# Two-layer mixed network on eight cores: the q/k normalisation and rotation of the last block issued one chunk later

## The reference

```python
h = shift_token(x)            # second half of the features delayed by one token
qkv = h @ wqkv
q, k, v = jnp.split(qkv, 3, axis=-1)
# to 8 heads of 64
q = l2norm(q) * qs            # l2norm(t) = t / clip(norm(t), 1e-12)
k = l2norm(k) * ksc
q, k = rotary_xpos(q, k)      # q * cos * scale + rotate_half(q) * sin * scale; k likewise with 1/scale
o = local_attention(q, k, v)  # window 512
```

## Time and profile before

| what | us |
|---|---|
| median of 2 runs | 26131.15 (26050.67 and 26211.63) |
| the profiled execution | 26278.76 |
| its span, slowest core (core 3) | 26277.2 |
| shortest core span of the same execution | 26008.6 |
| mean granted TensorE clock, slowest core | 0.615 of full |

### The profile page before, as it was taken

How to read it: one execution, slowest core, us unless ns; L and a number is a source line. 1 busy time by engine, 2 the same in 40 slices (tenths; PEclk the granted TensorE clock), 3 DMA queues, 4 the chain that set the end, 5 groups by cost and what they waited for, 6 DMA issues and landing times.

```text
span 26277.2 us, 172792 instructions; the slowest of 8 cores (26008.6 to 26277.2 us)
## 1 busy us (share of the span) xinstructions
PE 12685.6 (48%) x43266; PEld 5477.6 (21%) x43266; DVE 8884.8 (34%) x21875; ACT 4131.0 (16%) x6863; POOL 2171.6 (8%) x2737
## 2 busy tenths in 40 slices
PE   1212215771443344434443443444568777778773
PEld 0111112220111122222222222222211133211231
DVE  4444443334333333333333333332232222322222
ACT  0111111111212211111111111110123211233110
POOL 0010010000000000000000000000014300034000
PEclk7555557885666665555555555555775688755786
DMA  2111113333000010010001001001211101111103
GB/s 70 34 22 36 36 21 63 65 64 101 20 16 15 19 37 2 2 25 2 2 3 25 2 3 25 2 3 37 57 36 37 56 31 44 34 39 43 48 19 96
DMA packets 1067639, 849.03 MB, mean 32 GB/s; under 512 B 770196, under 2 KB 888756, under 8 KB 1064372
## 3 DMA queue, kind: packets, MB, share of 16 engines
q1 hardware_dynamic: 923572, 492.83, 7.8%
q0 software_dynamic: 143104, 345.14, 4.7%
HBM read 445.31 MB, written 302.25 MB: 28 GB/s over the span
## 4 chain that ended last, share of the span: by engine, by line
PE 45%; DVE 24%; issue 10%; ACT 8%; SPq 5%; DMA 5%; POOL 1%; DVEq 1%; another core or an unknown queue 0%; ACTq 0%; POOLq 0%; PEldq 0%
PE a_pU L1395 4%; PE ffc_pA L2175 3%; PE ffc_pG L2183 2%; PE ffc_pY L2203 2%; PE a_pZ L1388 2%; PE a_psQ L1162 2%; PE a_pJ L1390 2%; PE ffa_pP L1764 2%; DVE a_rrow L945 2%; PE a_psW L1167 2%; PE ffb_pO L1946 1%; DVE a_Gp L1392 1%; DVE a_phs L844 1%; PE ffb_pD L1948 1%; PE ffb_pS L1960 1%
## 5 line engine op out<-in xcount | busy, mean ns | idle before, releaser
L1395 PE MATMUL a_pU<-a_Zs,a_Hp 128*128 128x128 f32 x2560 | 980.5, 487 | 971.8 <-DVE a_Hp L1394 971.8
L1972 POOL TENSOR_TENSOR ffb_p<-ffb_e,ffb_mask 128x512 bf16<-128x512 bf16 x960 | 1093.1, 1150 | 965.2 <-ACT ffb_e L1966 523.2
L1449 ACT ACTIVATE a_sqO<-a_Osb 128x256 f32<-128x256 f32 x256 | 106.9, 418 | 6165.0 <-DVE a_Osb L1434 6070.2
L1395 PEld LDWEIGHTS a_pU<-a_Zs,a_Hp 128*128 128x128 f32 x2560 | 640.7, 311 | 1311.6 <-issue 1311.6
L1388 PE MATMUL a_pZ<-a_Gp,a_Hp 128*128 128x128 f32 x2560 | 845.7, 434 | 139.5 <-DVE a_Hp L1383 139.5
L2175 PE MATMUL ffc_pA<-ffc_hn,ffc_w 128*128 128x512 bf16 x2816 | 730.6, 407 | 295.6 <-DVE ffc_hn L2162 295.6
L1475 POOL DMA_DIRECT2D a_og<-a_OgB x256 | 137.9, 539 | 8393.1 <-DVE a_tE L1357 7180.0
L1390 PE MATMUL a_pJ<-a_Hp,a_Gp 128*128 128x128 f32 x2560 | 812.0, 421 | 0.0
L1397 DVE TENSOR_TENSOR a_Zs<-a_Zs,a_pU 128x128 f32<-128x128 f32 x1280 | 368.5, 288 | 1307.6 <-PE a_pU L1395 1299.4
L1964 DVE TENSOR_SCALAR ffb_cl<-ffb_pS 128x512 f32<-128x512 f32 x624 | 429.8, 691 | 957.1 <-PE ffb_pS L1960 565.2
L1946 PE MATMUL ffb_pO<-ffb_p,ffb_v 128*64 128x512 bf16 x960 | 597.0, 622 | 294.9 <-POOL ffb_p L1972 270.5
(11 more groups left out here) (395 smaller groups left out, 24637.6 us busy)
## 6 DMA issues: line engine op xcount, KB each, us to landing
moe_w<-l_w POOLq DMA_DIRECT2D x64, 1024.0 KB, 14.2
ln_x<-x SPq DMA_DIRECT2D x64, 512.0 KB, 3.8
a_phq<-a_phs SPq DMA_DIRECT2D x64, 512.0 KB, 3.8
f_xatt<-ffb_xo POOLq DMA_DIRECT2D x128, 256.0 KB, 2.3
ffc_w<-f_w SPq DMA_DIRECT2D x2, 11264.0 KB
ffc_x<-f_xatt SPq DMA_DIRECT2D x72, 256.0 KB, 4.5
xn_bf<-ln_o POOLq DMA_DIRECT2D x64, 256.0 KB, 2.3
s<-a_s POOLq DMA_DIRECT2D x32, 512.0 KB, 2.9
```

What stands on the lines that cost most here:

```text
L1395: zm = seq.step("tensor", lambda eng: nc.tensor.matmul(pU[:, 0:128], Hp[:], Zs[:], start=True, stop=True), deps=[he, zj, prev.get(("pU", 0))])
L1972: msk = seq.step("gpsimd", lambda eng, am=am, ma=ma: eng.tensor_tensor(psb[am][:], ebf[am][:], maskb[:, 512 * ma:512 * (ma + 1)], ALU.mult ...
```

## The change

The steps of a q/k chunk from the square to the store move into a function `emit_qk_tail`, and the loop calls it one chunk later: `mmR` and `mmS` of a chunk are called, then the tail of the chunk before, and the chunk's own arguments are kept in `pend_qk`. The tail of the tile's last k chunk is called after `mmR`, the copy and the store of the first v chunk. No instruction's operands, shape or number changes, and no buffer is added; what the tail's steps wait for stays as it was, with the counters `sb2` and `ao` advanced when the tail is called.

```diff
+        pend_qk = None
+        last_rot = None
...
             last_mm = None
             last_rot = None
+            def emit_qk_tail(pp, pp2, tb, scol, toff, oc, dst, t0, tld, mm_r, mm_s):
+                nonlocal pr_rw, pr_rv, pr_bc, pr_rotbb, pr_bbread, gsq, gao, last_rot
+                sb2 = gsq % 2; gsq += 1
+                sqs = seq.step("scalar", lambda eng, sb2=sb2, pp=pp: eng.activation(
+                    sqsb[sb2][:], psP[pp][:], AF.Square), deps=[mm_r] + list(pr_sqc[sb2]))
...
+                bc = seq.step("tensor", lambda eng: (
+                    nc.tensor.matmul(psBB[0:64, :], onesr[0:1, 0:64], rsA2[:], start=True, stop=True),
+                    nc.tensor.matmul(psBB[64:128, :], onesr[0:1, 0:64], rsB2[:], start=True, stop=True))[-1],
+                    deps=[rv, pr_rotbb])
...
+                rot = seq.step("vector", rotk, deps=[bbe, mm_r, mm_s, tld, qsld, ini, pr_aost[ao]])
+                last_rot = rot
...
+                pr_ppc[pp] = (sqs, rot)
+                pr_pp2c[pp2] = (rot,)
...
             for kind in range(3):
                 for oc in range(4):
...
                         pr_ppc[pp] = (cpv,)
                         pr_aost[ao] = sto
+                        if pend_qk is not None:
+                            emit_qk_tail(*pend_qk)
+                            pend_qk = None
                         continue
...
                     mm_s = seq.step("tensor", mmS, deps=[xld, sh, wld] + list(pr_pp2c[pp2]))
-                    sb2 = gsq % 2; gsq += 1
-                    sqs = seq.step("scalar", lambda eng, sb2=sb2, pp=pp: eng.activation(
...
-                    pr_aost[ao] = sto
+                    if pend_qk is not None:
+                        emit_qk_tail(*pend_qk)
+                    pend_qk = (pp, pp2, tb, 2 * kind, 1024 * kind, oc,
+                               qr_d if kind == 0 else kr_d, t0, tld, mm_r, mm_s)
             pr_rhs[tb] = last_mm
             pr_tblread[tb] = last_rot
```

More of the change, by code:

```diff
@@ L1755, in emit_l1ffn, with rotk @@
             last_rot = None
+            def emit_qk_tail(pp, pp2, tb, scol, toff, oc, dst, t0, tld, mm_r, mm_s):
[3 more added lines that the diff above has]
+                    sqsb[sb2][:], psP[pp][:], AF.Square), deps=[mm_r] + list(pr_sqc[sb2]))
+                nm1 = seq.step("tensor", lambda eng, sb2=sb2: nc.tensor.matmul(
+                    psN[0:1, :], onesc[0:64, :], sqsb[sb2][0:64, :], start=True, stop=True),
+                    deps=[sqs, pr_rw])
+                nm2 = seq.step("tensor", lambda eng, sb2=sb2: nc.tensor.matmul(
+                    psN2[0:1, :], onesc[64:128, :], sqsb[sb2][64:128, :], start=True, stop=True),
+                    deps=[sqs, pr_rw])
+                rw = seq.step("scalar", lambda eng: (
+                    b.fence(eng, "s", eng.activation(rsA[:], psN[0:1, :], AF.Ln)),
+                    b.fence(eng, "s", eng.activation(rsB[:], psN2[0:1, :], AF.Ln)),
+                    eng.activation(rsA3[:], rsA[:], AF.Exp, scale=-0.5),
+                    eng.activation(rsB3[:], rsB[:], AF.Exp, scale=-0.5))[-1],
+                    deps=[nm1, nm2, pr_rv, pr_rw])
+                rv = seq.step("vector", lambda eng: (
+                    eng.tensor_scalar(rsA2[:], rsA3[:], 1e12, None, ALU.min),
+                    eng.tensor_scalar(rsB2[:], rsB3[:], 1e12, None, ALU.min))[-1], deps=[rw, pr_bc])
+                bc = seq.step("tensor", lambda eng: (
+                    nc.tensor.matmul(psBB[0:64, :], onesr[0:1, 0:64], rsA2[:], start=True, stop=True),
+                    nc.tensor.matmul(psBB[64:128, :], onesr[0:1, 0:64], rsB2[:], start=True, stop=True))[-1],
+                    deps=[rv, pr_rotbb])
+                bbe = seq.step("scalar", lambda eng: eng.activation(
+                    bbS[:], psBB[:], AF.Copy), deps=[bc, pr_bbread])
+                ao = gao % 2; gao += 1
+                def rotk(eng, pp=pp, pp2=pp2, ao=ao, tb=tb, scol=scol, toff=toff):
+                    b.fence(eng, "v", eng.scalar_tensor_tensor(
+                        tw[0][:], psP[pp][:], qscol[:, scol:scol + 1], bbS[:], ALU.mult, ALU.mult))
+                    b.fence(eng, "v", eng.scalar_tensor_tensor(
+                        tw[1][:], psP2[pp2][:], qscol[:, scol + 1:scol + 2], bbS[:], ALU.mult, ALU.mult))
+                    b.fence(eng, "v", eng.tensor_tensor(
+                        tw[2][:], tw[0][:], tbl[tb][:, toff:toff + 512], ALU.mult))
+                    b.fence(eng, "v", eng.tensor_tensor(
+                        tw[3][:], tw[1][:], tbl[tb][:, toff + 512:toff + 1024], ALU.mult))
+                    return eng.tensor_tensor(aob[ao][:], tw[2][:], tw[3][:], ALU.add)
+                rot = seq.step("vector", rotk, deps=[bbe, mm_r, mm_s, tld, qsld, ini, pr_aost[ao]])
+                last_rot = rot
+                sto = seq.dma("gpsimd_dma", lambda eng, ao=ao, oc=oc, t0=t0, dst=dst: eng.dma_start(
+                    dst[128 * oc:128 * (oc + 1), t0:t0 + QT], aob[ao][:]), deps=[rot], n=1)
+                pr_ppc[pp] = (sqs, rot)
+                pr_pp2c[pp2] = (rot,)
+                pr_sqc[sb2] = (nm1, nm2)
+                pr_rw = rw
+                pr_rv = rv
+                pr_bc = bc
+                pr_rotbb = bbe
+                pr_bbread = rot
+                pr_aost[ao] = sto
```

## The result

The changed kernel takes 26815.67 us (median of 11 runs, 26699.35 to 27032.41) against 26204.64 us for the kernel before (median of 10). The ratio is 1.0244 with a 95% interval of 1.021 to 1.0278: slower by 2.4%, 611 us. The forecast was 26837 us.

What follows compares the result with a forecast made beforehand. It saw work spread over many stages, no share deciding, the touched stage 6.7% of the span. 36.9 + 4.9 − 2.1 + 4.4 = 44.1 us per tile, × 8 tiles × 2 layers = 706; 26131 + 706 = 26837 us, range 26640 to 27020.

Steps and rivals of the forecast that it cites:

- What bounds the stage: q/k/v projection, two layers, 6.7% of the span: TensorE waits 3.8 us per q/k chunk for the clamp, 1.8 us per tile for rotation.
- what the change could hide: Between a chunk's norm and broadcast matmuls nothing is put, so the 3.8 us wait stays 128 times; gain 0.
- What it uncovers: With two PSUM buffers, matmuls wait bare for the previous chunk's copy and rotation: 7 × 5.27 = +36.9 us per tile.
- The end of the tile: First v chunk's matmuls (3.5 us) and copy (about 1.4 us) come ahead of the last k chunk's tail: +4.9 us per tile.
- The clock: Matmul speed of a tile's q/k chunks after the second: +4.4 us per tile, between +0 and +1.45 us per chunk.
- −2.1 for u1: The tile's second q/k chunk runs without a stop at full clock, 3.45 us instead of 5.59: −2.1 us per tile.
- +4.4 for u2 to u7: Matmuls of the tile's third to eighth q/k chunks slow by 0.74 us each after longer stops: +4.4 us per tile.
- Queues and loads: GpSimd stores and SyncE loads: buffers are free chunks earlier and loads go out a tile ahead; cost 0.
- One sign of being wrong: Outside the stage's two windows: the prediction is wrong if the other stages change by more than 100 us.
- That the clock would stay low for all of M, N and B: Projection, norm and broadcast matmuls of the third to eighth q/k chunks at 1.2 GHz: +886 us, 27017 us; 13%.
- it would stay high: Projection matmuls of the third to eighth q/k chunks at full clock: +430 us, 26561 us, +1.6%; 7%.
- That a readout of PSUM costs TensorE nothing: Rotation reading PSUM does not hold up the next matmuls, so the 36.9 falls away: +115 us, 26246 us; 5%.

Runs made afterwards that it cites:

- e6: Changed kernel reordered: next chunk's matmuls, this chunk's broadcast, next chunk's norm; two buffers, freed after the rotation's second instruction, clamp before its last; 25799 us, ratio 0.9855.
- e8: e6 with the buffers given back by the rotation's fifth instruction again, as in the changed kernel; 26293 us, ratio 1.0018 to the kernel before.
- e1: Changed kernel, order kept, with three buffers instead of two for psP and for psP2, the norm rows sharing one bank; 26280 us, ratio 1.0012 to before.
- e2: Changed kernel with the rotation cut in two, PSUM buffers given back after its second VectorE instruction, not its fifth; 26627 us, ratio 1.0182 to before.
- e3: Kernel before, order untouched, with each chunk's matmuls also waiting for the rotation of the chunk just before; 26770 us, ratio 1.0225.
- e4: Changed kernel with the last k chunk's tail called ahead of the first v chunk; 26772 us, ratio 1.0223 to the kernel before.
- e9: e6 with three buffers, a repeat run of the same kernel; 25650 us, ratio 0.9748 to the kernel before.

## Why the prediction was right, point by point

**What bounds the stage; what the change could hide.** Right. The clamp's wait is 491.7 us after 492.5; gain 0, as read from the order. e6 and e8 show the other half of it: only matmuls placed between N and B take that wait away.

**What it uncovers.** Right, and the main term: 7 × 5.27 per tile. The waits measure 654.5 / 128 = 5.11 us, a little under the one in the earlier trace rows that served as price. e1 takes this wait away by a buffer, e2 shortens it by the release, e3 makes it alone, and each moved the stages by that much to within 16, 17 and 42 us.

**The end of the tile.** Right: 4.9 us per tile were forecast, and the waits give 4.7. The wait at v1 went from 1.8 to 5.1 us, 3.3 for v0's 3.5, and the new wait for the square is 22.1 us, 1.4 per tile as computed. e4 took 142 us out of the 163 that the two terms give.

**The clock.** This is the term that was mis-sized. The prediction had −2.1 for u1 and +4.4 for u2 to u7, +2.3 us per tile, 37 us in all. Measured on the slowest core of either, TensorE's busy time fell by 16 us, −1.0 us per tile. That sign rests on the pair of cores compared. The second layer of the core of before ran at 0.72 and took 872 us; on six other cores of the same execution its clock was 0.77 to 0.79 and it took 842 to 848 us. Core 5, for one:

```profile
22193.30:23035.80 842.50, 580.51 (x1792) 173.66 (x1792) 276.95 (x448) 244.56 (x416) 50.82 (x95) 0.79 0.10 33
```

The median busy time over the six cores whose matmul records are complete went from 1173 to 1181 us, +8, or +0.5 per tile. Either way the term was far too large. The prediction also took the clock to move between two levels; on the core of the earlier trace rows the trace of the second layer has 272 us at a third, 0.81 (last section).

Two parts of the term can be seen. M of u2 to u7 is 3.57 + 2.27 to 2.65, 6.0 us on average in one tile of either layer, not 6.33; the 5.59 us of before came from one tile of layer 0, and in the tile of layer 1 that begins at 22523.82 the same seven chunks average 5.88 us, so there the rise was 0.1 us and the gain of u1 2.4. And B became cheaper, which the prediction had not looked for: the groups of instructions, kernel before and then the changed one (busy us, mean ns of one | idle before):

```profile
L1807 PE MATMUL ffa_pB<-ffa_rA,ff_onesr 1*64 1x512 f32 x256 | 193.9, 848 | 492.5 <-DVE ffa_rB L1805 492.5
```

```profile
L1779 PE MATMUL ffa_pB<-ffa_rA,ff_onesr 1*64 1x512 f32 x256 | 163.4, 723 | 491.7 <-DVE ffa_rB L1777 491.7
```

In the trace before, the granted clock fell to 0.5 within B in 86 of the 128 chunks and stayed up to its end in 19; in that of the changed kernel it fell within B in 60 and stayed up in 38, to fall in the 5.1 us stop that follows, where nothing runs. N took back part of it, 643 ns a record after 613. Why the fall comes later is not shown: in e3, with stops as long, B became dearer (937 ns) and M cheaper (`ffa_pQ` from `ffa_x` 425 ns after 478). The granted clock of the stage fell from 0.78 and 0.72 to 0.69, as forecast, and TensorE's work still took hardly longer: much of the low clock lies in the stops.

**Queues and loads.** Right: no store and no load beyond the two at the stages' starts is among TensorE's waits.

**The sum.** 706 us were forecast for the stage, 632 measured: 21 us too much in the waits (669 against 648) and 53 in the clock. The whole moved by 611 us, 95 less than forecast. That 26837 us is only 21 us off is luck: the 26131 us that it starts from, the median of two runs, lies 74 us under the 26205 of ten. One sign of being wrong that the prediction had set came true: the time outside the two windows moved by −176 us, over its 100. It says nothing of the mechanism, since that time scatters by 208 us between kernels; the sign was set tighter than the scatter.

**The rivals.** That the clock would stay low for all of M, N and B (+886 us) and that it would stay high (+430) both fail on the rows: M starts low (3.57 us for eight matmuls) and rises within it (2.27 to 2.65 us for the next eight), in u2 to u7 of both tiles read. The rule of the Trainium skill (TensorE: Matmul & The Clock Gate, "HAM oscillation — how this bites in real kernels") that a burst after a wait starts at the half clock holds for M here, 3.57 us for its first eight matmuls, and for B in only part of the chunks: at its start, after the 3.8 us wait, the granted clock was down in 30 of 128. That a readout of PSUM costs TensorE nothing (+115) is e1, where a third buffer makes it true, and not the changed kernel.

## What to carry to other kernels

Issuing a chunk's tail one chunk later overlaps something only if the next matmuls come to stand between two dependent steps on the in-order engine, and only if a buffer is free for them: write the new list of that engine down and count how many chunks each PSUM buffer is held. Here the late order held each buffer one chunk longer with two of them, and it cost one rotation per chunk. With the matmuls between norm and broadcast and a release at the last reading instruction the same idea gained 1.5% (e6), and with a third buffer beside both 2.5% (e9); with that order and the late release it gained nothing (e8). A release on the last instruction of a step and not on the last one that reads was worth 2.4 us in each of 128 chunks.

## What the runs showed of the hardware that I had not expected

**A third rate of TensorE.** In e9 there are stretches with a granted clock of 0.81 and TensorE busy all the time. The windows of layer 0 (columns as above):

```profile
18900.00:18950.00 50.00, 50.00 (x183) 15.28 (x182) 24.70 (x49) 23.87 (x41) 4.86 (x9) 0.81 0.23 66
...
19000.00:19050.00 50.00, 44.30 (x186) 14.76 (x184) 28.25 (x55) 24.38 (x42) 5.41 (x10) 0.97 0.31 69
```

Inside the first, in order of time, four matmuls of 512 columns start 1.05 us apart:

```profile
18928.37 1.22 PE L1831 MATMUL ffa_pP<-ffa_x,ffa_wqkv 128*128 128x512 bf16 x4
18929.42 1.23 PE L1831 MATMUL ffa_pP<-ffa_xs,ffa_wqkv 128*128 128x512 bf16 x4
18930.47 1.22 PE L1854 MATMUL ffa_pQ<-ffa_x,ffa_wqkv 128*128 128x512 bf16 x4
```

The full level takes 0.86 us and the low one 1.71. 0.86 / 1.05 is 0.82, about the granted share. The level does not need a stage without stops: on the slowest core of the kernel before, in the second layer, there is such a stretch with TensorE busy for 11.8 of 16.5 us.

```profile
22850.80:22867.30 16.50, 11.81 (x44) 4.35 (x44) 1.44 (x3) 4.73 (x9) 2.70 (x5) 0.81 0.50 164
```

It came on some cores and not on others. In that layer of before cores 2 and 3 had 263 and 272 us of it and the other six none; in the second layer of e9 cores 0 and 1 had 72 and 93 us, cores 2 and 3 444 and 433, and cores 4 to 7 none. The two stages of e9 took 961 to 968 us on the cores without it and 990 to 1003 on the others, so it costs e9 some 30 us. The Trainium skill has this case (TensorE: Matmul & The Clock Gate, Part 1, the note on the peak-current limiter): 13/16 of the clock, 0.81, for the whole die once three cores of it run dense matmuls. The number agrees. That the whole die has it at once the traces do not bear out, as far as its cores start together: cores 0 and 1 had none of it in that layer of before. No run here varied the number of cores, so the cause is not shown.

**What a longer stop does to TensorE's own work.** From the kernel before to e3 the stops for a buffer grew by 641 us and the busy time fell by 43 us; in the changed kernel, with 626 us more, it moved by −16 us on the slowest core and +8 by the median of six. From e6 to e8 they grew by 365 us and the busy time rose by 147. In the kernel before 106 of 129 stretches of M began at the granted clock 0.5 already, and in the changed kernel all 129 did, so little was left to lose; in e6 it was 29 of 145, and with the stops of e8 it was 129 of 145. In these runs a longer stop cost more than its own length where the work behind it had begun at the full level before.
